# Rebuilding the expert tail of a fused attention and mixture-of-experts kernel

## Reference

```python
h = layernorm(x) * (1 + ca) + sa
x = x + ga * attn(h)                 # softmax over 16 heads, output projection
h = layernorm(x) * (1 + cb) + sb
x = x + gb * ffn(h)

# ffn, for each batch
nx = rmsnorm(X, g1)                  # 4 query heads of 64, shared keys and values
out = softmax(Q @ Kc.T * scale) @ Vc @ Wo.T
X = X + out
xf = rmsnorm(X, g2)
rw = softmax(xf @ Wr.T + expert_bias)          # 8 experts
topw, topi = top_k(rw, 2); topw = softmax(topw)
shared = (silu(xf @ sW1.T) * (xf @ sW3.T)) @ sW2.T
special = sum over the two chosen e of topw_e * ((silu(xf @ eW1[e].T) * (xf @ eW3[e].T)) @ eW2[e].T)
return X + shared + special
```

## Time and profile before

| what | value |
|---|---|
| median of 3 runs | 1429.34 us (1428.95 to 1434.13) |
| the profiled execution | 1428.52 us |
| its span, first to last instruction | 1426.5 us |
| mean granted clock of TensorE | 0.963 of full speed |
| PE busy | 1266.6 us, 89% of the span |
| DVE busy | 1071.2 us, 75% |
| ACT busy | 905.3 us, 63% |
| POOL busy | 353.8 us, 25% |

### The profile page before, as it was taken

The page is one execution under the profiler, slowest core; times in us unless marked ns, Lnnn a source line. Parts: engine busy times, 40 slices in busy tenths (PEclk is TensorE's granted clock), DMA queues, the critical chain, the costliest instruction groups (busy, mean ns, idle before and its releaser), DMA issues.

```text
span 1426.5 us, 18520 instructions
## 1 busy us (share of the span) xinstructions
PE 1266.6 (89%) x5896; PEld 901.3 (63%) x5896; DVE 1071.2 (75%) x2044; ACT 905.3 (63%) x1482; POOL 353.8 (25%) x381
## 2 busy tenths in 40 slices
PE   4777668999999999999999999999867799999994
PEld 2334534666666666666665667766535687888783
DVE  4956766988888787888878888889833757547688
ACT  2355765777877767766787766777636756555451
POOL 0443431112211212111212201111272001723346
PEclk9999888999999999999999999999988899999998
DMA  5000018000000000000000001001020423556644
GB/s 200 8 1 30 30 61 293 4 8 5 5 8 5 8 5 5 4 8 4 9 5 5 8 5 57 8 4 30 19 88 24 148 66 102 200 156 179 183 124 148
DMA packets 61375, 80.69 MB, mean 57 GB/s; under 512 B 12002, under 2 KB 51682, under 8 KB 61026
## 3 DMA queue, kind: packets, MB, share of 16 engines
q1 hardware_dynamic: 36384, 46.81, 10.1%
q0 software_dynamic: 10752, 21.18, 5.3%
q10 hardware_dynamic: 14146, 11.52, 2.4%
HBM read 41.79 MB, written 37.62 MB: 56 GB/s over the span
## 4 chain that ended last, share of the span: by engine, by line
PE 61%; DVE 15%; ACT 8%; POOL 5%; issue 4%; DMA 4%; ACTq 1%; POOLq 0%; SPq 0%; DVEq 0%
PE PS L1819 8%; PE PS L1748 7%; PE PS L1751 7%; PE PS L1765 6%; PE PS L1768 6%; PE PS L1766 6%; PE PS L1716 6%; DVE mx L1161 4%; PE PS L1845 4%; DVE PL L1190 3%; POOL xbuf L1540 2%; PE PS L1702 2%; POOL y L1552 2%; PE PS L1803 1%; PE PS L1729 1%
## 5 line engine op out<-in xcount | busy, mean ns | idle before, releaser
L783 ACT ACTIVATE PT<-PS 128x1024 f32<-128x1024 f32 x256 | 262.5, 1026 | 193.8 <-PE PS L1751 193.4
L1161 DVE TENSOR_REDUCE mx<-PS 128x1 f32<-128x512 f32 x512 | 336.6, 684 | 63.0 <-PE PS L1716 62.1
L1190 DVE TENSOR_TENSOR PL<-PT,PH 128x1024 fp32r<-128x1024 f32 x256 | 314.8, 1230 | 17.0 <-ACT PH L786 16.5
L786 ACT ACTIVATE PH<-PT 128x1024 fp32r<-128x1024 f32 x256 | 271.6, 1061 | 8.1
L1765 PE MATMUL PS<-PH,VH 128*65 128x512 f32 x512 | 214.9, 420 | 2.1 <-ACT OZ L795 2.1
L1768 PE MATMUL PS<-PL,VH 128*65 128x512 f32 x512 | 205.0, 400 | 11.7 <-DVE PL L1190 11.6
L1766 PE MATMUL PS<-PH,VL 128*65 128x512 f32 x512 | 203.9, 398 | 0.0
L1716 PE MATMUL PS<-KA,Q 128*128 128x512 f32 x384 | 153.0, 407 | 10.9 <-DVE mx L1161 7.0
L1748 PE MATMUL PS<-Q,KA 128*128 128x512 f32 x384 | 129.2, 418 | 3.1 <-DMA Q<-mT 3.1
L1751 PE MATMUL PS<-Q,KB 65*128 65x512 f32 x384 | 121.8, 398 | 0.0
L1768 PEld LDWEIGHTS PS<-PL,VH 128*65 128x65 f32 x512 | 70.3, 137 | 64.5 <-DVE PL L1190 15.3
(11 more groups left out here) (243 smaller groups left out, 2503.2 us busy)
## 6 DMA issues: line engine op xcount, KB each, us to landing
xbuf<-xT SPq DMA_DIRECT2D x26, 384.0 KB, 4.5
xg<-xbuf SPq DMA_DIRECT2D x78, 128.0 KB, 2.2
ybuf<-yo ACTq DMA_DIRECT2D x78, 128.0 KB
nxT<-in_wexp SPq DMA_DIRECT2D x9, 768.0 KB, 4.4
x<-in_x SPq DMA_DIRECT2D x8, 512.0 KB, 11.9
x_scratch<-x SPq DMA_DIRECT2D x2, 2048.0 KB, 6.8
Z<-z_scratch POOLq DMA_DIRECT2D x32, 128.0 KB, 3.3
nxT<-x_scratch SPq DMA_DIRECT2D x32, 128.0 KB, 3.5
```

The lines of the kernel that those rows point to most:

```text
L783: act.activation(PT[:, gs % 4, :], PS[:, bk:bk + 2, :].rearrange("p a n -> p (a n)"), ACT.Exp, scale=0.125).then_inc(sem("pt"), 1)
L786: act.activation(PH[:, gs % 4, :], PT[:, gs % 4, :], ACT.Copy).then_inc(sem("pt_h"), 1)
L1161: dve.tensor_reduce(mx[:, qb % 2, i, c:c + 1], PS[:, k, :], AX, ALU.max).then_inc(sem("dve_out"), 1)
L1190: dve.tensor_tensor(PL[:, gs % 4, :], PT[:, gs % 4, :], phf[:, gs % 4, :], ALU.subtract).then_inc(sem("pl"), 1)
```

## The change

The tail's order and its helpers are changed.

1. `TILES` begins with batch 2's shared tiles and ends with batch 1's.
2. Batch 2's router reads the tile's own high and low parts (`xh`, `xl`) against a split `wr2`; `rl_turn` is gone for it. Every normalised tile is made by ACT and stored to a DRAM scratch `nrm`: by POOL's queue for batch 1 (in the loop), by SP's for batch 2.
3. `scatter` no longer scales on DVE. `scatter_load` reads the tile back from `nrm` into `sx`: on POOL's queue for batch 1, on SP's for batch 2. The order is load, nothing, scatter, staged by one tile each, so that on POOL `load(i)` stands right behind `scatter(i-3)`, whose buffer it fills.
4. The last block of queries (block 31) isn't normalised: `proj_last` multiplies `OZ` with its row of sums by a 65x257 matrix and DVE divides after it; `proj_even` adds the other head's half in the loop. `z_out`, `z_inv`, `z_back` of block 31 are gone.
5. Eight `norm` jobs of batch 2 move into the loop.
6. `gb` is applied ahead: DVE multiplies a routed result by it while copying it out of PSUM (`down`), in 7 buffers; POOL makes X2 = X2*gb + x four tiles at a time (`t_mul`, `t_add`, 128x1024 each, eight times over both batches); the shared second weight is rescaled for batch 1. `finish` has two DVE instructions left and POOL's sums are gone from it.
7. `split_down`'s low part moves from DVE to POOL. Results are stored by SP's queue. Routed tiles are fetched 7 places ahead into 6 buffers.

```diff
-TILES = ([(None, i) for i in range(NT)] + [(0, i) for i in range(NTI)] + [(1, i) for i in range(NTI)]
-         + [(None, NT + i) for i in range(NT)])
+TILES = ([(None, NT + i) for i in range(NT)] + [(0, i) for i in range(NTI)] + [(1, i) for i in range(NTI)]
+         + [(None, i) for i in range(NT)])
 def scatter_jobs(b):
-    return [("scatter", b, i) for i in range(NT)]
+    return staged(NT, ("scatter_load", "rest", "scatter"), b)
+def total_jobs(b):
+    return [(name, b, g) for g in range(4) for name in ("t_mul", "t_add")]
 def tail_order():
-    side = [(-2, 9, [("z_out", 7, 3)] + last[0]),
-            (0, 1, [("z_inv", 7, 3), ("z_back", 7, 3)]),
-            (3, 9, last[1] + norm[8:]),
-            (4, 2.5, [j for ex in range(NE) for j in split_jobs(ex)]),
-            (5, 2.5, rlog_jobs(1)),
-            (25, 1, route_jobs(1, 5) + scatter_jobs(1)),
+    side = [(-3, 9, proj_jobs(3, 2) + [("norm_root", 1)]),
+            (-2, 9, [("proj_last", 12 + i) for i in range(4)]),
+            (-2, 2, norm + [("norm_root", 2)]),
+            (0, 1, [("rl_mm", 1, i) for i in range(NT)]),
+            (0, 1.55, [j for ex in range(NE) for j in split_jobs(ex)]),
+            (1, 0.5, total_jobs(0)),
+            (2, 1, [("rescale", 0)]),
+            (10, 1, [("rescale", 1)]),
+            (17, 1, [("rescale", 2), ("rescale", 3)]),
+            (17, 0.8, total_jobs(1)),
+            (17, 1, route_jobs(1, 4)),
+            (31, 3.6, scatter_jobs(1)),
             (NT + NTI + 3, 0.5, combine_jobs(0)),
-            (NT + 2 * NTI + 1, 1, combine_jobs(1))]
+            (NT + 2 * NTI + 1, 1.2, combine_jobs(1))]
...
# POOL
+        def scatter_load(b, i):
+            if b:
+                return
+            r = i % NSX
+            pe_of(w, ("q_mm", 1, 1, 3, 0))
+            w.wait_ge(*kept(token(0, i)))
+            if i >= NSX:
+                w.wait_ge(sem(f"d_sx{r}"), 32 * (i // NSX))
+            pool.dma_start(sx[:, r, :], nrm[0, i]).then_inc(sem(f"d_sl0_{r}"), 16)
+        def t_add(b, g):
+            ts = slice(b * NT + 4 * g, b * NT + 4 * g + 4)
+            w.wait_ge(sem("d_xo"), 16 * (4 * b + g + 1))
+            after_last("t_x2")
+            pool.tensor_tensor(X2[:, ts, :], X2[:, ts, :], xo[:, :, :], ALU.add).then_inc(sem("t_x2"), 1)
+        def split_down(ex):
+            k = order.index(ex)
+            hi, lo = (wsh, wsl) if ex == NE else (wh[:, ex, :, :], wl[:, ex, :, :])
+            w.wait_ge(sem("w_hi"), 3 * k + 3)
+            after_last("w_down")
+            pool.tensor_tensor(lo[:, :, 512:768], wst[:, k % 2, :, 512:768], hi[:, :, 512:768].bitcast(F32),
+                               ALU.subtract).then_inc(sem("w_down"), 1)
...
# PE
+        def proj_last(i):
+            w.wait_ge(sem("d_late"), 32)
+            w.wait_ge(sem("o"), 32)
+            k = bank("proj_last", i, 0)
+            pe.matmul(PS[:, k, 0:257], OZ[:, (i - 12) * P:(i - 11) * P], wol, start=True,
                       stop=True).then_inc(sem("pe_use"), 1)
         def rl_mm(b, i):
...
+                for dc in range(2):
+                    pe.matmul(PS[:, k, 0:2 * NE], xh[:, i % 3, dc, :], wr2[:, dc, :], start=(dc == 0), stop=False)
+                    mm = pe.matmul(PS[:, k, 0:2 * NE], xl[:, i % 3, dc, :], wr2[:, dc, :], start=False, stop=(dc == 1))
```

More of the change, by code:

```diff
@@ L130, in norm_jobs @@
 def norm_jobs(b):
-    return [("norm", b, i) for i in range(NT)] + [("norm_root", b)]
+    return [("norm", b, i) for i in range(NT)]
 def rlog_jobs(b):
@@ L167, in loop_order @@
     for pair in range(4):
-        for qb in range(4 if pair < 3 else 2):
+        for qb in range(4 if pair < 3 else 3):
             at = 192 * pair + 96 + 24 * qb + 48
             projections += spread(proj_jobs(pair, qb), at, at + 78 if pair < 3 else at + 23)
+    projections = [x for x in projections if x[0] < 8 * 96]
+    projections += spread([("proj_even", i) for i in range(12, NT)], 7 * 96 + 60, 7 * 96 + 90)
+    projections.sort(key=lambda x: x[0])
     for bh in range(8):
@@ L435, in _build @@
     banks.turn = 0
-    for s in range(-2, NTL + 3):
+    for s in range(-3, NTL + 3):
         for job in TAIL[s]:
@@ L498, in nx_free, with kept, token @@
             b, i = divmod(n - NNX, NT)
-            pe_of(w, ("nx_turn" if b < 2 else "rl_turn", b % 2, i, 0))
+            if b < 3:
+                pe_of(w, ("nx_turn" if b < 2 else "rl_turn", b % 2, i, 0))
+            else:
+                w.wait_ge(sem("tx"), i + 1)
+            if b >= 2:
+                w.wait_ge(*kept(n - NNX))
+    def kept(n):
+        b = n // NT - NB
+        return sem(f"d_nrm{b}_{n % NNX}"), 16 * sum(m % NNX == n % NNX for m in range(token(b, 0), n + 1))
+    def token(b, i):
+        return NB * NT + b * NT + i
     shared = [s for s in range(NTL) if TILES[s][0] is None]
@@ new lines, in fetch @@
+            experts_free(w)
+            keys_free(w)
+            pe_of(w, ("proj_last", NT - 1, 0))
+            if m >= NXR:
+                w.wait_ge(sem("tx"), s - NXR + 1)
+            if g is None:
+                for k in range(NNX):
+                    w.wait_ge(*kept(token(0, NT - 1 - k)))
+                src = nrm[0, i]
+            else:
+                for r in range(NSX):
+                    w.wait_ge(sem(f"d_sx{r}"), 32 * scattered(g, r))
+                w.wait_ge(sem("d_zero"), 16 * 26)
+                src = xbuf[g][i * P:i * P + P, :]
@@ L622, in _ @@
             load_x(g)
-        work = {"spill": spill, "max_turn": max_turn, "load_w": load_w, "split_down": split_down, "gather": gather,
-                "finish": finish}
+        work = {"spill": spill, "max_turn": max_turn, "load_w": load_w, "split_down": split_down, "finish": finish,
+                "scatter_load": scatter_load, "t_add": t_add, "rescale": rescale}
         run(work, FRONT)
@@ L822, in chooser @@
         def chooser(b):
-            for step in range(20):
+            for step in range(22):
                 if step == 2:
@@ L1546, in gather @@
             experts_free(w)
[L1547 removed]
+            for r in range(NYO):
                 w.wait_ge(sem(f"d_y{r}"), 16 * stored(b, r))
+            w.wait_ge(sem("w2h"), 1)
+            w.wait_ge(sem("w2l"), 1)
             if n >= NG:
@@ L1570, in _ @@
         work = {"add_bias": add_bias, "dots": dots, "shift2": shift2, "minus_one": minus_one, "k_mm": k_mm,
-                "q_hi": q_hi, "z_out": z_out, "z_back": z_back, "scatter": scatter, "gather": gather, "finish": finish}
+                "q_hi": q_hi, "z_out": z_out, "z_back": z_back, "scatter": scatter, "split_down": split_down,
+                "gather": gather, "rl_scale": rl_scale, "scatter_load": scatter_load, "t_mul": t_mul, "t_add": t_add}
         run(work, FRONT)
```

406 lines of the change are left out of this document (238 added, 168 removed), and 2 rows, old and new, of the table READERS.

## The result

The changed kernel takes 1454.55 us (median of 4 runs, 1451.92 to 1457.23) where the kernel before takes 1429.89 in the same comparison: a ratio of 1.016, 95% interval 1.0137 to 1.0183. It is slower, and lies 15.6 us above the upper end of my range (1405 to 1439). The profiled execution has a span of 1455.4 us, against 1426.5.

A forecast was written before the change was run, and what follows sets the result against it. POOL's own list was taken to bound the tail's start and its gathers the end. Differences over six stretches, from +15.2 us at the start, summed to -4.6: 1428.5 became 1423.9, plus 0.8 gave 1424.7 us; range 1405 to 1439.

The forecast's parts named there:

- the cycle of POOL's scatters at the start: At the loop's end, POOL's waits for landings make block 30's product end 15.2 us later.
- POOL's lag in tiles 0 to 16: In the first shared tiles, POOL falls behind PE with the weight splits, adding 3.6 us.
- The cycle of 4.6 us: At the loop's end, two scatters, the landing and a load's issue take 4.6 us in place of 2.6.
- POOL is free at 1025.6: At the loop's end, POOL finishes block 29's `z_back` at 1025.6 us, then starts six scatter cycles.
- A bound of mine: Loss at the tail's start if each load also delays the next scatter by a second landing: 32.7 us.
- the short one: Rival: POOL's scatter cycles at the loop's end take 3.5 us, block 30's product only 2 us later, 1411.5 us; chance 0.12.
- On 31 to silu 0: From block 30's product on POOL to the first shared tile's silu: 10.5 us in place of 7.5.
- the weight buffers absorb about 3: In tiles 0 to 16, buffer slack hides about 3 of the 6.6 us that POOL falls behind.
- splits paced by POOL and the loads: Rival: in tiles 0 to 16 experts' loads wait for POOL; 68 us, 1437.2 in all; chance 0.16 with late scatters.
- my "no gain" bound: Upper bound for tiles 0 to 16, each expert waiting for POOL and then its load: 64 us.
- 48 + 3.9: Tiles 0 to 16 without POOL's lag: 16 places of 3.0 us, plus 3.9 for early norms and a root.
- 8 x 0.9 + 1.5 = 8.7: In the choosing, eight POOL sums each hold DVE's list by about 0.9 us, plus 1.5 for fuller places.

The follow-up runs named there:

- loads on SyncE: The changed kernel with batch 1's scatter_load issued by SyncE instead of POOL: ratio 0.9928 to the kernel before (1.0028 on the slower chip).
- the same edit alone: The changed kernel with only one edit, all 16 products and sums ahead starting at place 15: ratio 1.0158 to the kernel before.
- small sums: POOL's products and sums on 1 column of 256: on the changed kernel 1473.1 us (slower chip), with batch 1's scatter loads on SyncE too 1397.3 us.
- the moved sums: Two kernels with all products and sums from place 15: over SyncE loads, four-piece sums and ScalarE stores, ratio 0.9862; on the changed kernel, 1.0158.
- the sums from 15: The changed kernel with SyncE loads, sums cut in four, ScalarE stores, and all products and sums starting at place 15: ratio 0.9862 to the kernel before.
- pieces: The changed kernel with each of POOL's products and sums of 1024 issued as four of 256: ratio 1.0072 to the kernel before.
- the last kernel: The changed kernel with SyncE loads, sums cut in four from place 11, ScalarE stores, and batch 2's scatter jobs at 3 a place: 1399.92 us, ratio 0.9787.

## Why the prediction was wrong, point by point

Two terms of the sum failed: the cycle of POOL's scatters at the start, put at 15.2 us of loss and measured at 28.3, and POOL's lag in tiles 0 to 16, put at 3.6 us and measured at 12 to 14. They make 22 of the 33.5 us by which the span was missed; the rest is in the choosing, the root and the end.

**The start of the tail: right mechanism, size off by 13.1 us.** The load's wait for a landing is the cause: taken off POOL's list, it gives 27.6 us back, all of the loss at that mark. Three terms of the sum were too small.
- The cycle of 4.6 us is 5.12 undisturbed (1047.30 to 1052.42). The landing is waited for 1.98 us where I took 1.46 from DVE's release in the earlier trace rows: the right number for DVE, not for POOL (more below). The rest of the parts held (0.98, 0.96, 0.57, 0.3 between).
- Some cycles have a scatter of 1.6 to 2.1 us in place of 1.0, so that twelve cycles and `z_out` took 1029.45 to 1097.79 = 68.3 where I had 58.6: +9.7.
- "POOL is free at 1025.6": I started block 29's `z_back` at once behind DVE's inverse of the trace before (1018.6). It began at 1022.71, after a wait for that inverse, which itself came later: +3.8 at 1029.45. The way from `z_back` to the product's end was 6.5 instead of 7.0.

A bound of mine (32.7 if each load cost a second landing) held the truth of 28.3; the number chosen did not, and the range for the whole kernel took little of it. That was the second mistake: I gave the long chain no case, only the short one.

**On 31 to silu 0:** +2.4. The root (1.3 for its table, 0.3), and then 2.88 us for DVE's reciprocal before the first scaling; I had let more of it overlap. This cost stays in every kernel of the study (12.7 in that with loads on SyncE).

**Silu 0 to 16: the step that failed is "the weight buffers absorb about 3".** I had worked out rounds of 14.2 against 12 us, took 3.6 us for the lag, and called a round of over 17 the rival that decides. The rounds were 15.1 and 15.6 us, 1 us off and well under 17, and POOL waited 6.2 to 6.7 us for x where I took 6. The parts of the round were nearly right, then. What was wrong is that slack would hide it: the load of x and the load of weights are in one queue, each waits for POOL in turn, and what stands behind them (the stores that ACT waits for, 10.6 us) stops as well. Against the kernels whose sums are moved away, the lag is 14 us on the first page (64.2 to 50) and 12.0 for the same edit alone (62.3 to 50.3). The rival *splits paced by POOL and the loads* had the mechanism right, though its 68 us did not come: 64.2 did, my "no gain" bound. The small sums (53.6 and 53.8) and the moved sums (49.8 and 50.3) show it. In the stops the granted clock fell too: PE was busy for 27.8 us in tiles 8 to 16 of the kernel after at 0.89, and for 24.3 at 1.00 with the sums from 15. My sum has no term for that, here or in the choosing. My 48 + 3.9 for everything but the lag is 51.9, against 50: that part held.

**Silu 16 to 94: off by 6.6 us; each hold was nearly right, what followed it was left out.** I put 8 x 0.9 + 1.5 = 8.7. Nine sums held VectorE's instructions for 10.1 us, 1.1 each. But between tiles 16 and 34 small sums win 13.7 us against the kernel after (62.84 to 49.16) and pieces 11.2, so a sum costs the stretch 1.5 us. The difference lies behind the held instruction: the router's list is a chain, the tiles' own instructions stand behind it, PE stops, and its clock falls. My upper bound, every sum holding DVE for its full length, was 18.9, and the truth lies between. The rest is a stall of some 3 us in tiles 44 to 49, where batch 2's scatters and the fetches meet; in the last kernel it is gone.

The Trainium skill, page "SBUF — State Buffer", section "SBUF: two separate sides", says that the lock lasts for a whole instruction and concerns VectorE's instructions that have two SBUF inputs or run in a two-port mode. The runs agree on the first kind: 2.47 us beside an instruction of 2.36, 0.71 beside pieces of some 0.7, while a reduction stays at 0.37 and an instruction with one input in PSUM (L1463 at 1194.99) at 0.41. The CAST of 1.34 us and the instruction of the earlier trace rows have one tensor as input and were held; they would belong to the second kind, and no run shows in which mode they ran.

**Tiles 52 to 94: right.** They take 106.5 us in every kernel of the changed form on the faster chips, and 114.7 to 115.2 before; I had put 8.4 us there. **The end: mostly right.** Gathers follow each other in 1.25 us; but DVE's steps hold POOL a few times (1.26 us once) and from the last gather to the end it is 10.4 where I had 8.8. From silu 94 on, the gain is 6.0 to 7.9 us and not 8.8.

So what the change was to bring is there: on one chip, 16.6 us from tile 52 on (115.2 + 63.1 against 106.5 + 55.2). It is paid for with 27.8 at the start, 7.4 in the choosing and 3.2 in tiles 34 to 52, and what else the new order should have won in tiles 0 to 16, 13 us, goes into the ring.

## What to carry to other kernels

A transfer's wait belongs on a queue that has nothing else on its list just then: the same load cost 28 us on the engine that also carries the chain of the softmax sums, and nothing on SyncE. If the wait must stay there, put other work of that engine in front of it: one word less in the staging gave 27 of these 28 us back. When two engines and a queue each wait for the other in a fixed order, count the round through all of them, not the busy time of each; two places of slack in the weight buffers didn't help against a round of 15 us where 12 were needed. A stop of PE can cost more than its length: behind the one of 3.08 us above, matmuls of 0.40 us took 0.63. Long GpSimd instructions beside a chain of short VectorE ones should be cut in pieces, or put where VectorE mostly reads PSUM (an instruction with an input there stays at 0.41 us beside a sum).

## What was not expected of the hardware

How long a scatter's landing is waited for depends on who waits. From the end of the second transfer on POOL's list, POOL itself goes on after 1.98 us (12 times within 0.02) and DVE in the kernel before after 1.45 to 1.48 us (five times between 1055.9 and 1067.9). SyncE, in the kernel with the loads on its queue, goes on after 1.51 to 1.74 us. The transfers are the same; why POOL sees them 0.2 to 0.5 us later was not tried.

Chips differ by more than some of these effects. The kernel with loads on SyncE took 1460.92 us on one and 1420.61 on another, the kernel before 1457.0 and 1430.24. Up to tile 34 both give the same stretches within 1.5 us. Then the slower one has spacings of up to 8.5 us between silus, in tiles 34 to 46, once at 59 and again from 97 on, mostly where scatters and gathers run. The waits from 1210 us on, tile 34 and the following, on the slower chip (line, what it waits for: us in all, times, longest) hold, among others,

```profile
POOL xbuf L1643 <- DMA nxT<-norm_scratch: 13.9, 4, 6.2
ACT xh L953 <- remote: 12.2, 4, 4.7
```

and on the other

```profile
POOL xbuf L1643 <- DMA nxT<-norm_scratch: 2.6, 3, 1.3
```

So POOL waits up to 6.2 us for a load of 128 KB there. Four waits of ACT there end on something that the profile calls remote. Whether it is the queues or the memory stays open, and one slower chip is no rule for chips.
